# Weight mixing, the recurrent stage and the projections of a two-layer decoder as one program over shared buffers

## The chip, the cores and the metric

The kernel runs on one core of one Trainium2 chip. The metric is the device time of one execution in microseconds, lower is better. A core has five engines with an instruction stream each: PE (TensorE), DVE (VectorE), ACT (ScalarE), POOL (GpSimd) and SP (SyncE), which here does nothing but issue DMAs. The engines run side by side and wait for one another through semaphores.

## The reference

The reference is a decoder of two layers on `x` of 8 batches x 512 rows x 256 columns, all in float32. Each layer has three parts, and after each part comes `x = layernorm(x + part(x))`. Only the first layer's first two parts matter here:

```
# part 1: recurrence with weights mixed per batch
xn      = x * rsqrt(mean(x*x) + 1e-6) * norm_weight
probs   = softmax(mean(xn over rows) @ router_w.T + router_b)       # 8 experts, per batch
W_hg    = sum_e probs[e] * w_hg[e]    (512 x 256)                    # mixed weights, one set per batch
W_out   = sum_e probs[e] * w_out[e]   (256 x 256)
hidden, gate = split(xn @ W_hg.T)
h_t     = sigmoid(-gate_t) * h_(t-1) + sigmoid(gate_t) * g(hidden_t)  # scan over 512 rows
x1      = layernorm(x + (h @ W_out.T + x))
# part 2: cross attention, 16 heads of 16 columns; ctx is a second input
q, k, v = x1 @ Wq.T + bq, ctx @ Wk.T + bk, ctx @ Wv.T + bv
scores  = softmax(q k^T / 4); the 52 keys with the smallest column sums are dropped; out = scores v
```

Behind these come a routed feed-forward part and the whole second layer. They are not touched.

## The kernel before

The kernel is a row of stages. Each stage is a block with one instruction stream per engine. A stage allocates its buffers and semaphores through `Room` (line 25); when the stage ends, `Room.clear` frees the semaphores and puts a barrier over all engines, so nothing of the next stage starts before everything of this one, its last store included, is done.

**Mixing** (`stage_mix`, line 65). SP loads the eight batches of `x` into `x_all` and then twelve pieces of 512 KB of expert weights into `chunk` (L116). ACT forms the sums of squares, POOL the inverse roots `inv_all`, PE the means, and a small chain of tiny operations gives the router's shares. Then PE multiplies each weight piece with the shares (L213, 12 pieces of 8 matmuls), DVE (L182) and ACT (L129) copy the halves into `w_all`: the mixed weights of all batches, 128 partitions x 8 batches x 2 x 768.

**Recurrent stage** (`stage_rec`, line 217). It builds its own identity matrix, and copies the mixed weights of two batches at a time by DMA from `w_all` into `whg` and `wout` (L269, L272). ACT first issues eight stores of 1 MB of zeros into the scratch `buf` (L310) and then comes to its first work, `turned(0)` (L316). The engines then go through the batches in a written order, with a hardware loop for batches 2 to 5. For batch b, PE does: 8 matmuls for gate and hidden (L412, "gate(b)" in this text), 8 transposes of the next batch's normalized rows (L399, "turn(b+1)"), 8 matmuls for the output of the batch before (L423, "output(b-1)"). ACT does three sigmoids (L324 to L326) and copies the transposed rows out of PSUM (L316). DVE does: maximum (L347), the sum with `x` of batch b-1 (L352), product (L358), statistics (L362), scan (L370), variance (L376, L379), normalized rows of batch b+2 (L337), and the final layernorm of batch b-1 (L386). SP stores `x1` (L287).

**Projections** (`stage_proj`, line 444). SP loads the three weights and their biases and the first two batches of `x1` and of `ctx` (L469 to L477). For batch b, PE does: 8 transposes of the rows (L564), Q and K with 4 matmuls each (L571, "Q(b)", "K(b)"), V with 8 (L576, "V(b)"). ACT copies the transposed rows (L522), and writes Q and K in full and as a bf16 part (L529, L530) and later the middle bf16 part of the rest (L534). DVE subtracts: the rest (L544) and the low part (L547), and adds the bias to V (L550). SP, in a loop, waits until V(b) is done, loads the rows and the context of batch b+2, then waits for the low parts and stores Q and K (768 KB each, L482) and V (512 KB, L485). All of these go through SP's one DMA queue.

**Attention and routing** (`stage_attend_route`, line 659). Heads go by in chunks of four. `half_chunk` (line 760) loads a chunk's queries or keys with six DMAs of 64 KB (L765). SP issues the queries of chunk 0 and all of chunk 1, ACT the keys of chunk 0. PE waits for chunk 0 and for six constants of POOL, and then does the first scores (L1360). DVE waits for four fills of POOL first, and ACT's first `Exp` (L993) loads its table.

Of the kernel before, what the change touches and what calls it, by code (L numbers as in the profile page):

```python
# [14 lines left out]
P = 128  # L15
# [49 lines left out]
def stage_mix(nc, a, x_all, inv_all, w_all):  # L65

    KC = P // E
    C = 4  # L70
    G = 3 * D // (KC * C)
    with ExitStack() as ctx:
        r = Room(nc, ctx, "mix")
        junk = r.sb("junk", [P, B, T, D], BF16)
        ssq, msq = r.sb("ssq", [P, B, T]), r.sb("msq", [P, B, T])
        mhalf = r.sb("mhalf", [P, T])
        meanT = r.sb("meanT", [P, DH, B])
        nw = r.sb("nw", [P, DH])
        rwT = r.sb("rwT", [P, DH, E])
# [3 lines left out]
        prT = r.sb("prT", [E, B])  # L83
        prP = r.sb("prP", [P, B, 1])
        ident = r.sb("ident", [P, P])
        sel = r.sb("sel", [E, E, KC])
        mask = r.sb("mask", [P, KC])
        blocks = r.sb("blocks", [P, B, KC])
        chunk = [r.sb(f"chunk{g}", [P, C, D]) for g in range(G)]
        wide = r.sb("wide", [P, B, T, B])  # L90
        mean = r.sb("mean", [B, D])
        ps_sum = r.ps("ps_sum", [B, D])
        ps_mean = r.ps("ps_mean", [P, DH, B])
        ps_small = r.ps("ps_small", [P, 3, 8])
        ps_w = [[r.ps(f"ps_w{u}{h}", [P, C, B, KC]) for h in range(DH)] for u in range(2)]
        c_ld = r.sem("c_ld")
        x_ld, w_ld = [r.sem(f"x_ld{j}") for j in range(B // 2)], [r.sem(f"w_ld{g}") for g in range(G)]
        ssq_up, msq_up, inv_up, mean_up = (r.sem(n) for n in ("ssq_up", "msq_up", "inv_up", "mean_up"))
        const_up, soft_v, soft_s, soft_t = (r.sem(n) for n in ("const_up", "soft_v", "soft_s", "soft_t"))
        mixed, out_v, out_s = r.sem("mixed"), r.sem("out_v"), r.sem("out_s")  # L100
        wide_up = r.sem("wide_up")
# [3 lines left out]
        def _(sp):  # L105
# [9 lines left out]
            for g in range(G):  # L115
                sp.dma_start(chunk[g][:, :, :], a["L0_mix_w"][g].rearrange("p (c d) -> p c d", c=C)).then_inc(w_ld[g], 16)  # L116

        @block.scalar
        def _(act):
            for b in range(B):  # L120
# [5 lines left out]
            act.activation(ex[:, :], lg[:, :], ACT.Exp, bias=nmax[:, :], accum_out=esum[:, :]).then_inc(soft_s, 1)  # L126
            for g in range(G):
                act.wait_ge(mixed, g + 1)
                act.activation(w_all[:, :, 1, g * (C * KC):(g + 1) * (C * KC)].rearrange("p b (c k) -> p b c k", c=C),  # L129
                               ps_w[g % 2][1][:, :, :, :].rearrange("p c b k -> p b c k"), ACT.Copy).then_inc(out_s, 1)  # L130

        @block.gpsimd
        def _(pool):
            pool.memset(mhalf[:, :], -0.5).then_inc(const_up, 1)
            pool.memset(ident[:, :], 0.0).then_inc(const_up, 1)
            pool.memset(sel[:, :, :], 1.0).then_inc(const_up, 1)
            pool.wait_ge(const_up, 3)
            pool.affine_select(out=ident[:, :], in_=ident[:, :], compare_op=ALU.not_equal, fill=1.0, base=0,
                               pattern=[[-1, P]], channel_multiplier=1).then_inc(const_up, 1)

            pool.affine_select(out=sel[:, :, :], in_=sel[:, :, :], compare_op=ALU.is_equal, fill=0.0, base=0,
                               pattern=[[-1, E], [0, KC]], channel_multiplier=1).then_inc(const_up, 1)
            pool.memset(wide[:, :, :, :], 0.0).then_inc(const_up, 1)
            for b in range(B):
                pool.wait_ge(msq_up, b + 1)
                pool.tensor_tensor(inv_all[:, b, :], msq[:, b, :], mhalf[:, :], ALU.pow).then_inc(inv_up, 1)
# [2434 lines left out]
```

## Time and profile before

| | us |
|---|---|
| runs of the kernel before | 2081.13, 2084.89, 2091.33 (median 2084.89) |
| the profiled execution | 2084.87 |
| its span (first to last instruction in the trace) | 2083.1 |
| PE busy | 1843.2 (88%) |
| DVE busy | 1253.6 (60%) |
| ACT busy | 976.6 (47%) |
| POOL busy | 617.0 (30%) |
| moved by DMA | 189.5 MB |

The engines overlap, so the busy times don't add up to the span. The profiled execution's own time is 1.8 us above its span. The span begins with the mixing stage; the first scores of the attention stage are at 327.58 us, and everything behind them is some 1755 us of the span.

### The profile page before, as it was taken

What the parts mean: (1) busy time and instruction counts of PE and PEld (TensorE: products, weight loads), DVE (VectorE), ACT (ScalarE), POOL (GpSimd) and SP (SyncE); (2) the same over time, 40 slices, a digit from 0 to 9 for tenths busy, and PEclk for the clock granted to TensorE, in tenths of its full rate; (3) what the DMA queues carried; (4) which work ended last, traced back from release to release, by engine and by line L of the source; (5) the groups of instructions that cost most, each with busy time, mean ns of one, the idle gap of its engine ahead of it and who ended that gap; (6) DMA issues with size and microseconds to landing.
All of it is one profiled execution on the core that took longest, in us unless ns stands there. A gap on an engine that the chain in (4) does not pass through costs nothing. (4 is left out here: it accounts for less than half of the span.)

```text
span 2083.1 us, 26554 instructions
## 1 busy us (share of the span) xinstructions
PE 1843.2 (88%) x8441; PEld 1082.9 (52%) x8441; DVE 1253.6 (60%) x2929; ACT 976.6 (47%) x2530; POOL 617.0 (30%) x800
## 2 busy tenths in 40 slices
PE   7694885889988988889878999999689999999997
PEld 5352542445544545445445655656456565566553
DVE  2474444888899998999631121231566667675665
ACT  4230556998898989989322111111132223232210
POOL 2000004555576666766430001000433113211100
PEclk9897996999999999999999999999899999999999
DMA  5533554121222322221563344341421111100000
GB/s 202 218 110 94 206 206 99 53 62 51 67 77 65 88 62 82 75 76 59 185 211 111 101 133 139 112 142 51 142 62 50 48 39 46 46 5 21 11 11 21
DMA packets 168422, 189.50 MB, mean 91 GB/s; under 512 B 19908, under 2 KB 146107, under 8 KB 167264
## 3 DMA queue, kind: packets, MB, share of 16 engines
q1 hardware_dynamic: 160512, 162.90, 24.7%
q0 software_dynamic: 6144, 16.18, 2.5%
q10 hardware_dynamic: 1632, 8.78, 1.1%
q8 instruction: 66, 1.08, 0.2%
q14 instruction: 68, 0.56, 0.1%
HBM read 118.95 MB, written 63.18 MB: 87 GB/s over the span
## 5 line engine op out<-in xcount | busy, mean ns | idle before, releaser
L927 POOL TENSOR_SCALAR xa_probs<-xa_probs,xa_small 128x512 f32<-128x512 f32 x512 | 344.7, 689 | 253.0 <-DVE xa_small L1083 253.0
L993 ACT ACTIVATE xa_probs<-xa_ps_s,xa_small 128x512 f32<-128x512 f32 x512 | 360.8, 742 | 46.2 <-DVE xa_small L1089 41.3
L1089 DVE TENSOR_REDUCE xa_small<-xa_ps_s 128x2 f32<-128x1024 f32 x256 | 309.2, 1208 | 52.4 <-PE xa_ps_s L1360 52.3
L1371 PE MATMUL xa_ps_t<-xa_ident,xa_probs 128*128 128x128 f32 x2048 | 309.1, 284 | 17.2 <-DVE early L756 7.1
L1371 PEld LDWEIGHTS xa_ps_t<-xa_ident,xa_probs 128*128 128x128 f32 x2048 | 230.1, 143 | 153.1 <-ACT early L758 44.4
L2425 PE MATMUL ta_ps_e<-late,ta_x5T 128*128 128x512 f32 x512 | 243.9, 612 | 1.4 <-DVE ta_acc L2175 1.4
L1360 PE MATMUL xa_ps_s<-xa_k,xa_q 96*128 96x512 bf16 x512 | 159.8, 395 | 77.9 <-ACT xa_probs L993 56.2
L2175 DVE SCALAR_TENSOR_TENSOR ta_acc<-ta_ps_e,ta_gate,ta_acc 128x256 f32<-128x256 f32 x256 | 123.6, 483 | 101.4 <-PE ta_ps_e L2425 95.2
L1621 ACT ACTIVATE ex_hid<-ex_ps_g 128x512 f32<-128x512 f32 x64 | 38.2, 597 | 274.2 <-PE ex_ps_u L1718 271.3
L1672 DVE TENSOR_TENSOR ex_hid<-ex_hid,ex_ps_u 128x512 f32<-128x512 f32 x64 | 44.0, 688 | 182.6 <-ACT ex_hid L1621 177.1
L2425 PEld LDWEIGHTS ta_ps_e<-late,ta_x5T 128*128 128x128 f32 x512 | 98.5, 197 | 102.3 <-issue 87.4
L758 ACT ACTIVATE early<-xa_ps_t 128x512 f32<-128x512 f32 x216 | 135.4, 653 | 8.1 <-PE xa_ps_t L1371 7.8
L758 ACT ACTIVATE late<-xa_ps_t 128x512 f32<-128x512 f32 x216 | 133.9, 653 | 10.9 <-PE xa_ps_t L1371 10.8
L993 ACT ACTIVATION_READ_ACCUMULATOR xa_probs<-xa_ps_s,xa_small 128x1 f32 x512 | 133.7, 261 | 0.0
L1718 PE MATMUL ex_ps_g<-ex_xsT,early 128*128 128x512 f32 x256 | 120.4, 592 | 2.1 <-ACT ex_xsT L1603 2.1
L1718 PE MATMUL ex_ps_u<-ex_xsT,early 128*128 128x512 f32 x256 | 120.3, 592 | 0.0
L1360 PEld LDWEIGHTS xa_ps_s<-xa_k,xa_q 96*128 96x128 bf16 x512 | 35.6, 99 | 153.8 <-ACT xa_probs L993 92.3
L1728 PE MATMUL ex_ps_d<-early,ex_hid 128*128 128x256 f32 x512 | 113.4, 379 | 0.1
L1728 PEld LDWEIGHTS ex_ps_d<-early,ex_hid 128*128 128x128 f32 x512 | 96.0, 190 | 13.3 <-DVE ex_hid L1672 0.5
L1865 POOL DMA_INDIRECT ta_rows<-scratch_results,route_i x56 | 55.2, 985 | 90.7 <-POOLq L34 74.8
L1718 PEld LDWEIGHTS ex_ps_u<-ex_xsT,early 128*128 128x128 f32 x256 | 48.6, 190 | 61.2 <-issue 61.2
L1683 DVE COPY ex_out<-ex_ps_d 128x1024 f32<-128x1024 f32 x16 | 19.6, 1225 | 98.4 <-PE ex_ps_d L1728 98.4
(355 smaller groups left out, 3044.5 us busy)
## 6 DMA issues: line engine op xcount, KB each, us to landing
xa_q<-scratch_qk_parts SPq DMA_DIRECT2D x192, 64.0 KB
xa_k<-scratch_qk_parts SPq DMA_DIRECT2D x186, 64.0 KB
scratch_buf<-rec_zeros ACTq DMA_DIRECT2D x8, 1024.0 KB
early<-in_L_ffn_Wg SPq DMA_DIRECT2D x16, 512.0 KB
early<-in_L_ffn_Wu SPq DMA_DIRECT2D x16, 512.0 KB
early<-in_L_ffn_Wd SPq DMA_DIRECT2D x16, 512.0 KB
ex_xs<-scratch_buf SPq DMA_DIRECT2D x16, 512.0 KB, 5.2
scratch_results<-ex_out SPq DMA_DIRECT2D x16, 512.0 KB, 3.2
```

What stands on the lines that cost most here:

```text
L758: eng.activation(dst, src, ACT.Copy, accum_out=out).then_inc(copied[t], 1)
L927: ins = pool.tensor_scalar(probs[n % NP][:, t, :], probs[n % NP][:, t, :], rinv[n % 2][:, t:t + 1], 1.0, ALU.mult, ALU.mult)
L993: ins = act.activation(probs[n % NP][:, t, :], ps_s[j][:, t % 2, :], ACT.Exp, bias=nmax[n % 2][:, t:t + 1], accum_out=rsum[n % 2][:, t:t + 1])
L1089: dve.tensor_reduce(nmax[n % 2][:, 2 * j:2 * j + 2], ps_s[j][:, :, :], AX.X, ALU.max, negate=True).then_inc(max_up, 1)
L1360: ins = pe.matmul(ps_s[j][:, t % 2, :], q[c % 2][:, n % CH, t * P:(t + 1) * P], k_[c % 2][:, n % CH, :], start=True, stop=True)
L1371: ins = pe.transpose(ps_t[t % 2][:, i * P:(i + 1) * P], probs[m % NP][:, i, t * P:(t + 1) * P], ident[:, :])
L1672: dve.tensor_tensor(hid[m % 2][:, j, :], hid[m % 2][:, j, :], ps_u[j % 2][:, :], ALU.mult).then_inc(hid_up, 1)
L1718: ins = pe.matmul(ps[:, :], wt[:, h, j * P:(j + 1) * P], xsT[u][:, h, :], start=(h == 0), stop=(h == DH - 1))
L1728: ins = pe.matmul(ps_d[:, t, :], hid[u][:, j, t * P:(t + 1) * P], wd[u][:, j, :], start=(j == 0), stop=(j == FT - 1))
L1865: pool.indirect_dma_start(out=rows[b % 2][:, n, t, :], out_offset=None, in_=a["results"], in_offset=bass.IndirectOffsetOnAxis(ap=route_i[: ...
L2175: dve.scalar_tensor_tensor(acc[c % 2][:, t, :], ps_e[n % 2][:, i, :], gate[c % 2][:, t, e:e + 1], acc[c % 2][:, t, :], ALU.mult, ALU.add). ...
L2425: ins = pe.matmul(ps_e[n % 2][:, :, :].rearrange("p e d -> p (e d)"), x5T[c % 2][:, h, t * P:(t + 1) * P], ew[:, h, e:e + 2, :].rearrange( ...
```

## The change

`stage_mix`, `stage_rec` and `stage_proj` become one function, `stage_front`, with one block. The barriers and the clearing of semaphores between the three are gone, and the loops are written out batch by batch in Python, so every address is a constant. In detail:

- PE reads the mixed weights straight from `w_all`; the copies into `whg` and `wout` are gone. `late`, a buffer of 128 partitions x 64 KB that the later stages have anyway, holds the weight pieces first, and afterwards the projection's weights, rows, contexts and V. The bf16 parts and the full Q and K lie over `w_all`.
- `turn(0)`, its copy by ACT and a first `Sigmoid` for the table stand inside the mixing; rows 0 and 1 are normalized between the sums of squares.
- POOL fills the zeros after the mixing; SP, not ACT, stores them, 1 MB behind each store of `x1`.
- The projection's weights and the first two contexts are loaded after the mixing, the first two batches of rows behind the stores of `x1` of batches 2 and 3.
- PE's order at the seam is gate(7), output(6), turn_rows(0), K(0), output(7), Q(0), turn_rows(1), V(0); from then on K(b), Q(b), turn_rows(b+1), V(b). K goes before Q on ACT and DVE too.
- SP loads the context and the rows of batch b+1 (not b+2) just ahead of its stores of batch b, and so behind its stores of batch b-1. Behind the stores of batch 3 it loads the twelve pieces of the first query and key chunk of the attention stage (`ahead`).
- In the attention stage, chunk 0 is not loaded any more, ACT's table of `Exp` is loaded by a tiny activation, the wait of DVE for POOL's fills stands only before its first use, PE's wait for the constants before its first transpose, and POOL fills `vm` last.

The core of the diff (of `stage_front` only the parts that differ from the three stages; normalize to finish, rest, low and values do per batch what they did before):

```diff
+        chunk = [late[:, g * C * D:(g + 1) * C * D].rearrange("p (c d) -> p c d", c=C) for g in range(G)]
+        zeros = late[:, 12288:14336]
+        wq, wk, wv = (late[:, i * 512:(i + 1) * 512].rearrange("p (h n) -> p h n", n=D) for i in range(3))
+        ahead = first_chunk(late)
 @block.sync
+            def context(b):
+                wait(sp, pv_up, b - 1)
+                sp.dma_start(cT[b % 2], a["ctxT"][b].rearrange("(h p) s -> p h s", p=P)).then_inc(cT_ld[b % 2], 16)
+            def rows(b):
+                sp.wait_ge(x1_st[b % 2], 16 * (b // 2 + 1))
+                wait(sp, pt_up, b - 1)
+                sp.dma_start(x_in[b % 2], tok(a["x1"][b])).then_inc(x_in_ld[b % 2], 16)
+            def store(b):
+                sp.wait_ge(low_up, 2 * b + 2)
+                for n in range(2):
+                    sp.dma_start(a["qk_parts"][b, n]..., parts[n][b % 2]...).then_inc(qkv_st[b % 2], 16)
+                sp.wait_ge(v_up, b + 1)
+                sp.dma_start(tok(a["v"][b]), v[b % 2]).then_inc(qkv_st[b % 2], 16)
+            sp.wait_ge(mixed, G)
...
+            for b in range(2):
+                context(b)
+            sp.wait_ge(zero_up, 1)
+            for b in range(B):
+                sp.wait_ge(x1_up, b + 1)
+                sp.dma_start(tok(a["x1"][b]), x1[b % 2][:, :, :]).then_inc(x1_st[b % 2], 16)
+                sp.dma_start(buf[b], zeros).then_inc(zero_st, 16)
+                if b in (2, 3):
+                    rows(b - 2)
+            for b in range(B):
+                if b >= 1 and b + 1 < B:
+                    context(b + 1)
+                    rows(b + 1)
+                store(b)
+                if b == 3:
+                    sp.wait_ge(qkv_st[0], 48)
+                    for n in range(2):
+                        load_half(sp, a, ahead[n], 0, n, ahead_ld)
 @block.scalar
+            for b in range(B):
+                sigmoids(b)
+                if b + 1 < B:
+                    turned(b + 1)
...
+            rows_turned(0)
+            for b in range(B):
+                high(b, 1)
+                high(b, 0)
+                if b + 1 < B:
+                    rows_turned(b + 1)
+                middle(b, 1)
+                middle(b, 0)
 @block.tensor
+            for b in range(B):
+                gate(b)
+                if b + 1 < B:
+                    turn(b + 1)
+                if b >= 1:
+                    output(b - 1)
+            turn_rows(0)
+            project(0, 1)
+            output(B - 1)
+            for b in range(B):
+                if b >= 1:
+                    project(b, 1)
+                project(b, 0)
+                if b + 1 < B:
+                    turn_rows(b + 1)
+                project_v(b)
 stage_attend_route
-            half_chunk(sp, 0, 0)
             chunk(1)
-            pool.memset(vm[:, :, :, :, :], 0.0).then_inc(pad_up, 1)
-            half_chunk(act, 0, 1)
+            act.wait_ge(const_up, 1)
+            act.activation(warm[:, :], mhalf[:, 0:1], ACT.Exp)
-            dve.wait_ge(pad_up, 4)
-            pe.wait_ge(const_up, 6)
```

## Rows read from the trace of the kernel before

**Rows 1.** The page: busy time and instructions of each engine.
```profile
PE 1843.2 (88%) x8441; PEld 1082.9 (52%) x8441; DVE 1253.6 (60%) x2929; ACT 976.6 (47%) x2530; POOL 617.0 (30%) x800
```

**Rows 2.** Windows by stage: length, busy of each engine, PE clock, DMA share, GB/s.
```profile
29.00:53.80 24.80, 24.01 (x192) 23.82 (x192) 8.30 (x12) 7.16 (x12) 0.00 (x0) 0.90 0.12 47
53.80:67.66 13.86, 1.83 (x9) 1.49 (x9) 3.84 (x8) 1.39 (x3) 2.55 (x4) 0.64 0.84 330
67.66:185.10 117.44, 96.17 (x312) 56.54 (x312) 79.69 (x192) 32.05 (x39) 8.80 (x8) 0.94 0.31 118
185.10:202.75 17.65, 1.94 (x9) 1.57 (x9) 0.00 (x0) 1.23 (x2) 0.50 (x2) 0.50 0.68 201
202.75:311.30 108.55, 93.35 (x312) 55.47 (x312) 47.47 (x40) 61.12 (x87) 0.00 (x0) 0.97 0.56 194
311.30:327.58 16.28, 0.00 (x1) 0.04 (x2) 0.00 (x0) 1.28 (x1) 2.64 (x13) 0.50 0.89 191
```

**Rows 3.** Timeline, mixing's end to the second gate: start, duration, engine, line, operation.
```profile
53.06 0.69 DVE L182 COPY w_all<-mix_ps_w 128x512 f32<-128x512 f32 x1 [1.10 <-PE mix_ps_w L213]
57.43 8.77 ACTq L310 DMA_DIRECT2D scratch_buf<-rec_zeros  x8
67.66 2.90 PE L412 MATMUL rec_ps_h<-rec_xnT,rec_whg 128*128 128x512 f32 x3 [8.20 <-ACT rec_xnT L316]
76.67 1.03 ACT L324 ACTIVATE rec_val<-rec_ps_h 128x1024 f32<-128x1024 f32 x1 [7.85 <-PE rec_ps_g L412]
80.77 5.37 PE L412 MATMUL rec_ps_h<-rec_xnT,rec_whg 128*128 128x512 f32 x8 [3.27 <-ACT rec_xnT L316]
...
122.13 3.60 PE L412 MATMUL rec_ps_g<-rec_xnT,rec_whg 128*128 128x512 f32 x8
```

**Rows 4.** Timeline, the recurrent stage's end.
```profile
170.78 2.32 DVE L370 TENSOR_TENSOR_SCAN rec_h<-rec_keep,rec_val 128x512 f32<-128x512 f32 x2
173.20 5.68 PE L423 MATMUL rec_ps_o<-rec_wout,rec_h 128*128 128x256 f32 x16 [6.24 <-DVE rec_h L370]
183.64 1.38 DVE L386 TENSOR_SCALAR rec_x<-rec_z,rec_mv,rec_rstd 128x256 f32<-128x256 f32 x4 [1.12 <-POOL rec_rstd L302]
```

**Rows 5.** Timeline, the projections' last two batches and the first scores.
```profile
290.62 3.62 PE L576 MATMUL proj_ps_v<-proj_wv,proj_cT 128*128 128x256 f32 x16
293.25 1.07 ACT L534 ACTIVATE proj_partsq<-proj_restq 128x1024 bf16<-128x1024 f32 x1
294.07 1.04 PE L564 MATMUL proj_ps_t<-proj_ident,proj_x 128*128 128x128 f32 x8
295.63 1.00 ACT L522 ACTIVATE proj_xT<-proj_ps_t 128x1024 f32<-128x1024 f32 x1
300.30 3.60 PE L571 MATMUL proj_ps_k<-proj_cT,proj_wk 128*128 128x512 f32 x8
306.52 1.23 DVE L544 TENSOR_TENSOR proj_restk<-proj_fullk,proj_partsk 128x1024 f32<-128x1024 f32 x1 [2.21 <-ACT proj_partsk L530]
310.12 0.37 SPq L482 DMA_DIRECT2D scratch_qk_parts<-proj_partsq  x1
319.13 5.62 SPq L765 DMA_DIRECT2D xa_q<-scratch_qk_parts  x12
327.58 1.87 PE L1360 MATMUL xa_ps_s<-xa_k,xa_q 96*128 96x512 bf16 x4 [20.23 <-DMA xa_k<-scratch_qk_parts]
```

**Rows 6.** DMA issues of 188 to 330 us, with time to landing.
```profile
proj_x<-scratch_x SPq DMA_DIRECT2D x8, 512.0 KB, 4.0
```

**Rows 7.** One line (L116), the twelve weight pieces of 512 KB: time to landing.
```profile
DMA to landing us min/median/max: 11.9/13.0/14.5
```

**Rows 8.** Windows: one projection batch's transfers, the first chunks, low clock after idle PE.
```profile
170.80:177.00 6.20, 3.80 (x9) 3.11 (x10) 4.12 (x12) 0.00 (x0) 1.01 (x1) 0.50 0.00 0
217.50:226.10 8.60, 7.87 (x21) 3.95 (x22) 3.38 (x3) 3.80 (x7) 0.00 (x0) 1.00 1.01 360
321.00:327.60 6.60, 0.02 (x1) 0.06 (x2) 0.00 (x0) 1.28 (x1) 0.93 (x4) 0.50 1.18 139
```

More of the change, by code:

```diff
@@ L118, in _, with turned, sigmoids @@
         @block.scalar
         def _(act):
+            def turned(b):
+                act.wait_ge(t_up, b + 1)
+                wait(act, hg_up, b - 1)
+                for k in range(DH):
+                    ins = act.activation(xnT[b % 2][:, k, :], ps_t[:, k, :], ACT.Copy, scale=nw[:, k:k + 1])
+                ins.then_inc(xnT_up, 1)
+            def sigmoids(b):
+                act.wait_ge(hg_up, b + 1)
+                wait(act, h_up, b - 1)
+                act.activation(val[b % 2][:, :, :], ps_h[:, :, :], ACT.Sigmoid).then_inc(sig_up, 1)
+                act.activation(take[b % 2], ps_g[:, :, :], ACT.Sigmoid).then_inc(sig_up, 1)
+                act.activation(keep[b % 2], ps_g[:, :, :], ACT.Sigmoid, scale=-1.0).then_inc(sig_up, 1)
@@ L120, in _, with middle @@
+            def middle(b, n):
+                act.wait_ge(rest_up, 2 * b + 2 - n)
+                act.activation(parts[n][b % 2][:, 1, :, :], full[n][b % 2], ACT.Copy).then_inc(mid_up, 1)
             for b in range(B):
@@ L185, in _, with turn @@
+            dve.wait_ge(pc_ld, 96)
+            for b in range(B):
+                rest(b, 1)
+                rest(b, 0)
+                low(b, 1)
+                low(b, 0)
+                values(b)
         @block.tensor
         def _(pe):
+            def turn(b):
+                pe.wait_ge(xn_up, b + 1)
+                wait(pe, xnT_up, b)
+                for k in range(DH):
+                    for t in range(T):
+                        ins = pe.transpose(ps_t[:, k, t * P:(t + 1) * P], xn[b % 2][:, t, k * P:(k + 1) * P], ident[:, :])
+                ins.then_inc(t_up, 1)
@@ new lines, in gate @@
+            def gate(b):
+                pe.wait_ge(xnT_up, b + 1)
+                wait(pe, g_up, b)
+                wait(pe, sig_up, 3 * b)
+                if b == 0:
+                    pe.wait_ge(out_v, G)
+                    pe.wait_ge(out_s, G)
+                for out, first in ((ps_h, 0), (ps_g, DH)):
+                    for n in range(DH):
+                        for k in range(DH):
+                            ins = pe.matmul(out[:, n, :], w_all[:, b, k, (first + n) * P:(first + n + 1) * P], xnT[b % 2][:, k, :],
+                                            start=(k == 0), stop=(k == DH - 1))
+                ins.then_inc(hg_up, 1)
@@ new lines, in project @@
+            def project(b, n):
+                w, src, up = ((wq, xT[b % 2], q_up), (wk, cT[b % 2], k_up))[n]
+                if b == 0:
+                    pe.wait_ge(pc_ld, 96)
+                    pe.wait_ge(sig_up, 3 * B)
+                    pe.wait_ge(g_up, B)
+                if n == 0:
+                    pe.wait_ge(xT_up, b + 1)
+                else:
+                    pe.wait_ge(cT_ld[b % 2], 16 * (b // 2 + 1))
+                wait(pe, high_up, 2 * b - n)
+                for m in range(DH):
+                    for k in range(DH):
+                        ins = pe.matmul(ps_qk[n][:, m, :], w[:, k, m * P:(m + 1) * P], src[:, k, :], start=(k == 0), stop=(k == DH - 1))
+                ins.then_inc(up, 1)
@@ L187, in _, with project_v @@
+            def project_v(b):
+                if b == 0:
+                    pe.wait_ge(z_up, B)
+                wait(pe, v_up, b)
+                for t in range(T):
+                    for k in range(DH):
+                        ins = pe.matmul(ps_o[:, t, :], cT[b % 2][:, k, t * P:(t + 1) * P], wv[:, k, :], start=(k == 0), stop=(k == DH - 1))
+                ins.then_inc(pv_up, 1)
             pe.wait_ge(const_up, 6)
```

640 lines of the change are left out of this document (249 added, 391 removed).

## The prediction

> **What bounds the kernel now.** I read the page first, then windows by stage, then the timeline of the front, then the landings of its DMAs. On the page PE is busy 88% of the span [rows 1]; the attention and the later stages, some 1755 us, are not touched, so the question is how much of the front's 327.58 us is PE at work. The windows answer it [rows 2]. In the mixing PE is busy 24.0 of 24.8 us. From its end to the first gate matmul (13.86 us) it works 1.8 us; in the recurrent stage 96 of 117 us; from that stage's last layernorm to the first Q matmul (17.65 us) 1.9 us; in the projections 93 of 109 us; and from the last stores to the first scores (16.28 us) not at all. So three seams of 48 us together hold 3.8 us of PE's work. What ends each: at the first, ACT issues eight stores of zeros for 8.77 us before it copies the transposed rows [rows 3]; at the second, barrier, weight loads and row loads; at the third, the landing of the last stores, the barrier, and loads that end only at 327.58 [rows 5]. Inside the stages the loops run on PE and short waits.
>
> **The change part by part.** Times are in the trace's own span (2083.1 us; this execution took 2084.87, practically the median of 2084.89), and each step moves the chain.
>
> *First seam.* The last copy into `w_all` ends at 53.06 + 0.69 = 53.75. gate(0) then waits for nothing else: its rows are turned during the router chain, where PE and ACT idle. It starts at 53.8 and not 67.66: -13.9 us. It also starts right behind the mixing, at full clock. Before, gate(0) took from 67.66 to 76.6, its first matmuls 0.97 us each, against 2 x 3.6 = 7.2 us later, less 0.1 of overlap [rows 3]: -1.9 us. ACT's three sigmoids and the copy still stand between gate(0) and gate(1), so the dip of gate(1) (its first half 5.37 and not 3.60 us) may stay; I keep it, and count its 1.6 us as a bound. Sum -15.8 us.
>
> *The recurrent loop.* DVE's order per batch and PE's are the old ones, so the period stays. The 16 copies out of `w_all` fed nothing late; their removal is worth 0. The zero stores go to SP's queue: 1 MB at 360 GB/s [rows 8] is 2.9 us per batch of more than 12 us, hidden behind the loop; uncovered it would cost that much per batch, 23 us in all. The written-out code costs nothing: the mixing is written out already and PE is busy 24.0 of 24.8 us there [rows 2].
>
> *Second seam.* Scan(7) ended at 170.78 + 2.32 = 173.1 [rows 4], now 157.3. turn_rows(0) and K(0) fit in front of it. output(7) runs at full clock in 3.6 us, the duration of V, which has its shape [rows 5], and not in 5.7, which it took after 6.2 us of idle at half clock [rows 4, 8]: end 161.0. Then Q(0) to 164.6, turn_rows(1) to 165.6, V(0) 169.2, K(1) 172.8, Q(1) 176.4 (3.6, 1.04, 3.6 us [rows 5]). On DVE the last layernorm ended 6.1 us after output(7) (178.9 to 185.0 [rows 4]): 167.1. Two rests of 1.23 us: 169.6. From the end of the last rest to the store of Q and K it took 2.4 us (307.75 to 310.12 [rows 5]): store(0) is issued at 172.0.
>
> *A new loop.* Here the change adds a wait. SP issues in order, and rows(b+1) stands behind store(b-1). turn_rows(b+1) needs those rows; ACT's middle parts stand behind its copy of the turned rows; DVE's low parts need the middle parts; store(b) needs the low parts; rows(b+2) stands behind store(b). Waiting on PE behind turn_rows are V, the next K and Q. The old kernel loaded two batches ahead and before the stores. From turn_rows to its store: 1.04 + 1.00 + 1.07 [rows 5] + 2.4 + 0.3 for the hand-overs = 5.8 us. From the store's issue to the landing of the rows: the queue holds 768 + 768 + 512 KB of stores, then 512 KB of context, then the rows, 3.1 MB. The same 3.1 MB took 8.6 us before, with the DMAs fully busy (share 1.01) [rows 8]; what a load costs beside its bytes is 4.0 us, the landing of the rows on an empty queue [rows 6], less 1.4 us for 512 KB at 360 GB/s: 2.6. Sum 11.2, period 17.0 us, against 11.9 us of PE's work (3.6 + 3.6 + 1.04 + 3.62) and some 13 before (108.55 us for eight batches, the first partly at a low clock [rows 2]). In the gap of 5 us PE's clock may fall, as it did to 0.50 in the idle time before output(7) [rows 8]; turn_rows then takes about twice its 1.04 us, a period of 17.8 us. I take 17.2, a fall in one gap of four. Do the rows really wait for the bytes ahead of them? The twelve weight pieces of the mixing, as large as the rows and issued behind other loads, landed 11.9 to 14.5 us after their issue [rows 7], the rows on an empty queue after 4.0 [rows 6]. I take the queue as served in order. The bounds of the period are 11.9 (hidden) and 23.7 (PE at half clock throughout).
>
> The Trainium skill, "DMA: Bandwidth & Descriptors", section "Queues, rings and completion order", says that on each DMA engine the descriptors of one issuing engine's queue are consumed in ring order. It speaks against the change, and rows 7 agree; the sum by it is the one taken here, while 4.0 us as in rows 6 would give the first rival.
>
> So turn_rows(2) starts at 172.0 + 11.2 = 183.2, PE having stood since 176.4. Five more periods: 86.0. Ahead of context 5 and rows 5 the queue gets the first chunk, twelve DMAs in 5.62 us of issuing [rows 5], 786 KB at 139 GB/s [rows 8]: +5.7. turn_rows(7) is at 274.9. Behind it itself, V(6), K(7) and Q(7): 11.9 us, and 2.0 if 4 of them run at half clock: 288.8. The last matmul of Q or K ended at 303.90 and the store came at 310.12: 6.2, so 295.0. From there to the next stage 9.0 us as before (310.12 to 319.13 [rows 5]): 304.0.
>
> *Third seam.* The first scores find their chunk: 304.2, not 8.45 us after the stage's start. Of the 8.2 us saved the +5.7 above are given back. The table of `Exp` (ACT's 1.28 us in the last window [rows 2]) was covered by the load; its cover now is the first scores and DVE's maximum of them, so it costs 0, at most 1.28. PE's and DVE's waits for POOL's constants, which the load covered too, are moved behind the first scores: 0. Chunk 1 needs about the 8.45 us that chunk 0 needed; four heads, whose scores alone are 4 x 4 matmuls at 1.87 us per four, stand before its use: 0.
>
> Sum: 304.2 - 327.58 = -23.4 us; 2084.87 - 23.4 = **2061.5 us**. With full clock in the new loop (17.0 us, nothing at its end) the first scores are at 301.2, and with the dip of gate(1) gone at 299.6: 2056.9. With 17.8 us they are at 307.2: 2064.5. A start of the queue 0.5 us quicker or slower moves it by 3 us, a rate 10% lower by 5. The likeliest's own range is 2050 to 2072.
>
> **The rivals.**
> (a) *The row loads don't wait for the stores.* For it: the landing of 4.0 us [rows 6]; against: rows 7. The period is 5.8, then 2.3 until the rows are issued (four DMAs before them at 5.62/12 us each and a short wait for V's sum), then 4.0: 12.1; turn_rows(2) at 178.3, (7) at 178.3 + 60.5 + 5.7 = 244.5, the first scores at 244.5 + 11.9 + 6.2 + 9.2 = 271.8: 2029.1 us. Hidden entirely, at 11.9 us a period with turn_rows(2) at 176.4 and no charge for the chunk: 263.0, 2020.3 us.
> (b) *PE's clock.* The new gaps fall into every batch, and PE stays at half clock through Q, K, V and turn_rows: 23.7 us per batch, more than the DMA's chain. For it: after idle PE ran at 0.50 [rows 8], and gate(1) slowed too [rows 3]. Against: the window after the idle seam of 17.65 us averages 0.97 [rows 2], so full clock comes back under work. Then turn_rows(7) is at 183.2 + 118.5 = 301.7, the first scores at 301.7 + 23.7 + 6.2 + 9.2 = 340.8, +13.2: **2098.1 us, slower**. It decides from a period of about 21.5 us up.
> (c) *The change gives back what it takes.* The seams go, but the new loop costs 21 to 22 us a batch, because stores and loads that follow in one queue run below 360 GB/s (at 240 GB/s the 8.6 us are 13): 5 x 4.4 us more and 4.4 before the first, 2088 us, no change. Against: the same bytes ran at 360 before, mixed in the same way.
>
> **How the numbers follow.** Forecast 0.60, (a) 0.20, (c) 0.12, (b) 0.08. A measurement of this kernel tells a change from none at about 0.5%, 10.4 us, so faster means below 2074.5 and slower above 2095.3. The forecast's range and (a) lie below: faster 0.80, same 0.12, slower 0.08. The range runs from 2024 to 2078: it cuts off the hidden case, most of (c) and (b).
>
> **What would show it.** The first gate matmul near 54 us, at once at full clock; output(7) at 3.6 us. In the projections PE waits for a DMA of the rows before each turn_rows from batch 2 on, turn to turn 16 to 18 us, once about 23 (batch 5), and rows landing 7 to 9 us after their issue; with (a) they land after 4 and the period is near 12; with (b) the windows show a clock near 0.5 over the projections. First scores within 0.5 us of the stage's start, near 304 us. Everything behind it should keep its length (1755 us); if that grows, I am wrong about what the change touches.

## The result, and the profile after

The changed kernel takes 2057.26 us (median of four executions) against 2084.76 for the kernel before (2081.13 to 2091.33, four runs). Three of the four executions took 2056.47, 2057.01 and 2057.51 us; the fourth was disturbed and took 4657.62 us, and neither the ratio nor anything below rests on it. The ratio is 0.9875, with a 95% interval of 0.984 to 0.991. The whole interval lies below 1: the kernel is faster, by some 1.2%. The prediction was 2061.5 us, with 2024 to 2078 as its range.

The profiled execution of the changed kernel took 2057.51 us, its span 2055.5. The page's line of busy times answers to [rows 1].

```profile
PE 1844.1 (90%) x8441; PEld 1084.2 (53%) x8441; DVE 1249.7 (61%) x2929; ACT 976.9 (48%) x2532; POOL 615.1 (30%) x795
```

The same number of matmuls, the same busy time: the change computes nothing less, it moves work together. The windows of the front [rows 2], cut at the new seams (columns: window, length, busy time of PE, weight load, DVE, ACT and POOL with their instructions, PE clock, DMA share, GB/s):

```profile
29.00:51.76 22.76, 21.70 (x192) 21.54 (x193) 8.47 (x13) 8.60 (x14) 0.76 (x1) 1.00 0.06 22
51.76:148.81 97.05, 89.56 (x296) 52.05 (x297) 66.57 (x155) 30.98 (x39) 7.29 (x7) 0.96 0.33 113
148.81:173.40 24.59, 22.70 (x81) 13.59 (x79) 19.33 (x44) 11.31 (x16) 2.01 (x2) 1.00 0.61 230
173.40:275.54 102.14, 66.39 (x202) 41.58 (x201) 31.55 (x27) 41.19 (x59) 0.00 (x0) 0.85 0.60 184
275.54:294.73 19.19, 16.55 (x56) 11.04 (x56) 8.41 (x8) 9.75 (x13) 0.00 (x0) 0.91 0.33 110
294.73:303.66 8.93, 0.00 (x1) 0.03 (x2) 1.11 (x1) 0.04 (x1) 0.04 (x2) 0.65 0.71 235
```

Recurrent loop and seam are now one run of work right behind the mixing: from 51.76 to 173.40 PE idles some 9 us in 122. But in the fourth window, the new projection loop, PE works 66 of 102 us at a mean clock of 0.85. PE's own timeline says why (start, length, engine, line, operation, and in brackets the idle time before it and what ended it):

```profile
51.76 3.67 PE L467 MATMUL front_ps_h<-front_xnT,front_w_all 128*128 128x512 f32 x8 [0.83 <-DVE front_w_all L420]
62.96 6.55 PE L467 MATMUL front_ps_h<-front_xnT,front_w_all 128*128 128x512 f32 x8 [3.22 <-ACT front_xnT L260]
...
155.17 3.72 PE L476 MATMUL front_ps_o<-front_w_all,front_h 128*128 128x256 f32 x16 [1.89 <-DVE front_h L355]
...
169.92 3.60 PE L503 MATMUL front_ps_h<-late 128*128 128x512 f32 x8
181.34 1.97 PE L487 MATMUL front_ps_t<-front_ident,late 128*128 128x128 f32 x8 [7.82 <-DMA late<-scratch_x]
...
275.54 1.09 PE L487 MATMUL front_ps_t<-front_ident,late 128*128 128x128 f32 x8 [3.81 <-DMA late<-scratch_x]
276.47 5.30 PE L512 MATMUL front_ps_o<-late 128*128 128x256 f32 x16
...
303.66 1.87 PE L1337 MATMUL xa_ps_s<-late 96*128 96x512 bf16 x4 [11.56 <-PEq L34]
```

The first gate is at 51.76 instead of 67.66 [rows 3], output(7) at 155.17 instead of 173.20 [rows 4], the first scores at 303.66 instead of 327.58 [rows 5]. PE's waits between 150 and 303 us, by releaser (total, times, longest):

```profile
PE front_ps_t L487 <- DMA late<-scratch_x: 35.8, 6, 10.7
```

turn_rows(b) stands for the 8 transposes of the rows of batch b in the new projection loop. Every turn_rows from batch 2 on waits for its rows. turn_rows(2) to (7) start at 181.34, 199.23, 217.18, 239.29, 257.45 and 275.54: periods of 17.9, 17.95, 22.1, 18.2 and 18.1 us, where PE's work is 11.2 (measured in e5 below). The longest period is the one whose rows stand behind the first chunk. SP's queue in one period (L190 loads rows, L195 stores Q and K), and the chunk:

```profile
173.39 1.23 SPq L190 DMA_DIRECT2D late<-scratch_x  x1
187.73 0.95 SPq L195 DMA_DIRECT2D scratch_qk_parts<-front_w_all  x2
...
191.47 1.22 SPq L190 DMA_DIRECT2D late<-scratch_x  x1
...
224.99 8.64 SPq L88 DMA_DIRECT2D late<-scratch_qk_parts  x12
```

From turn_rows(2) to its store: 187.73 - 181.34 = 6.4 us. From there to turn_rows(3): 11.5 us. Of these 3.7 are issuing what stands ahead, and 7.8 are the landing of the rows, which was 4.0 us on an empty queue [rows 6].

### The profile page after: what moved, and what is told of

The parts are those of the page before. It is cut to its first block and busy times, and to the rows that moved or that the text cites. A ratio compares the mean times of both kernels' runs of the same rounds, so it can differ in the third digit from the quotient of the medians.

```text
span 2055.5 us, 26201 instructions
## 1 busy us (share of the span) xinstructions
PE 1844.1 (90%) x8441; PEld 1084.2 (53%) x8441; DVE 1249.7 (61%) x2929; ACT 976.9 (48%) x2532; POOL 615.1 (30%) x795
## 5 line engine op out<-in xcount | busy, mean ns | idle before, releaser
L1350 PE MATMUL xa_ps_t<-xa_ident,xa_probs 128*128 128x128 f32 x2048 | 309.9, 285 | 17.1 <-DVE early L736 7.1
L1337 PE MATMUL xa_ps_s<-xa_k,xa_q 96*128 96x512 bf16 x496 | 153.1, 391 | 53.2 <-ACT xa_probs L971 51.4
```

Of the source, the lines that this page charges most:

```text
L1337: ins = pe.matmul(ps_s[j][:, t % 2, :], q_[:, n % CH, t * P:(t + 1) * P], keys[:, n % CH, :], start=True, stop=True)
L1350: ins = pe.transpose(ps_t[t % 2][:, i * P:(i + 1) * P], probs[m % NP][:, i, t * P:(t + 1) * P], ident[:, :])
```

## The experiments

Nine kernels, e1 to e9, and the changed one once more (c_changed_again), in three groups: e1 to e4; the repeat and e5 to e7; e8 and e9. The kernel before was measured beside each group, with medians of 2079.71, 2080.43 and 2083.15 us, so a ratio compares better than two medians of different groups. No experiment puts one of the three seams back by itself: what each seam gave is read from the timelines, and the experiments are about the new loop, the clock and the written-out code. T2 and T7 stand for the starts of turn_rows(2) and (7); in the changed kernel T7 - T2 is 94.2 us, and in its second profile (c_changed_again) 94.7.

**e1: rows loaded two ahead.**
```diff
                 if b >= 1 and b + 1 < B:
                     context(b + 1)
-                    rows(b + 1)
+                if b + 2 < B:
+                    rows(b + 2)
                 store(b)
```


> The changed kernel, with SP issuing the load of rows(b+2) and not rows(b+1) ahead of the stores of batch b (the buffer is free by then). Theory (the new projection loop is bound by the row loads that stand in SP's queue behind the stores of the batch before): PE's waits for the row loads (35.8 us in six waits) go, turn_rows comes every 12 to 12.5 us instead of every 18.0; the context of batch 5 still stands behind the first chunk, so K(5) waits some 5 us. First scores at 268 to 272 us of the span instead of 303.7, the execution near 2022 to 2026 us. Rival 1 (the period is the sum of the DMA work and PE's clock, not the order): the period stays above 16 us, first scores above 290. Rival 2 (the context loads take the rows' place as the late ones): period 14 to 16, PE waits for the context before each K.

Measured: 2020.72 us, ratio 0.9716 (0.970 to 0.9733). No turn_rows waits any more; PE waits for the context instead (the wait between 155 and 241.3 us):
```profile
187.64 1.04 PE L488 MATMUL front_ps_t<-front_ident,late 128*128 128x128 f32 x8
PE front_ps_g L504 <- DMA late<-in_ctxT: 9.5, 3, 5.4
268.80 1.87 PE L1338 MATMUL xa_ps_s<-late 96*128 96x512 bf16 x4 [11.55 <-PEq L34]
```
T7 - T2 is 241.30 - 171.71 = 69.6 us against 94.2, and the first scores are 34.9 us earlier, 33.2 of it behind turn_rows(1). The period is 11.2 us only where no context is late, 13.9 on the mean, so the second rival holds in part: three contexts came late and not one. The forecast's mechanism is shown: the new loop's period is the wait of the rows behind the store. What is late next is the load that still stands behind it.

**e2: rows ahead of the context.**
```diff
-                    context(b + 1)
                     rows(b + 1)
+                    context(b + 1)
```


> The changed kernel, with the rows of batch b+1 issued ahead of its context (two lines of SP swapped). Theory (one queue, served in order): the rows lose one DMA of 512 KB in front of them, 1.4 us at 360 GB/s; the period falls from 18.0 to 16.6, first scores 6 x 1.4 = 8.4 us earlier, near 295.3, the execution near 2049. Rival (DMAs in flight share the bandwidth, the order doesn't matter): the rows land when all 3.1 MB have, period and first scores unchanged within 1 us.

Measured: 2039.8 us, ratio 0.9816 (0.980 to 0.9833); T7 - T2 is 85.8 us, 1.7 a batch less than 94.2. The first scores come at 290.35, 5 us earlier than expected, of which 3 lie ahead of turn_rows(0), where gate(1) has no slow half here. With 512 KB fewer ahead of them (1.4 us at the 360 GB/s of [rows 8]) the rows are that much earlier, as an order by bytes within one queue would have it. But this run does not show that order: SP also issues the rows 1.4 us sooner, because the issue of the context (1.36 us) no longer stands ahead, and from their issue they land after 7.0 to 8.2 us, outside the chunk's period, against 7.3 to 8.1 in the changed kernel. The shorter gap also lets the clock stay up in some gaps (turn_rows at 1.09 to 1.10 us in three of six):
```profile
185.24 1.31 SPq L190 DMA_DIRECT2D late<-scratch_x  x1
186.59 1.36 SPq L185 DMA_DIRECT2D late<-in_ctxT  x1
193.41 1.10 PE L487 MATMUL front_ps_t<-front_ident,late 128*128 128x128 f32 x8 [3.37 <-DMA late<-scratch_x]
230.50 1.97 PE L487 MATMUL front_ps_t<-front_ident,late 128*128 128x128 f32 x8 [9.63 <-DMA late<-scratch_x]
```

**e3: rows in POOL's queue.**
```diff
                     context(b + 1)
-                    rows(b + 1)
+            for b in range(2, B):                                    # on POOL
+                pool.wait_ge(v_up, b - 1)
+                pool.wait_ge(x1_st[b % 2], 16 * (b // 2 + 1))
+                wait(pool, pt_up, b - 1)
+                pool.dma_start(x_in[b % 2], tok(a["x1"][b])).then_inc(x_in_gp[b % 2], 16)
```


> The changed kernel, with the rows of batches 2 to 7 loaded by POOL's queue instead of SP's, released by the same events (V of the batch before the last summed, x1 stored, buffer read). Theory (the rows wait for what stands ahead of them in their own queue): in a queue of their own they land 4 to 6.5 us after issue although the same stores run, the period falls to 13 to 15.5 us, first scores at 282 to 290, the execution 2036 to 2044. Rival (it is the bytes of the DMA engines, whichever queue they come from): the rows land at about the same point, 16.5 to 18 us a period, first scores above 297.

Measured: 2031.01 us, ratio 0.9767 (0.9749 to 0.9785); first scores 280.71. PE then waits for the semaphore of that queue. Stores, context, rows and the turn they feed, in one period, and the row of the DMA issues of 172 to 253 us (count, KB, median to landing):
```profile
200.19 0.95 SPq L196 DMA_DIRECT2D scratch_qk_parts<-front_w_all  x2
201.68 1.24 SPq L199 DMA_DIRECT2D scratch_v<-late  x1
201.95 0.75 POOL L257 DMA_DIRECT2D late<-scratch_x  x1 [16.11 <-DVE late L390]
202.96 1.45 SPq L186 DMA_DIRECT2D late<-in_ctxT  x1
208.65 1.10 PE L495 MATMUL front_ps_t<-front_ident,late 128*128 128x128 f32 x8 [1.40 <-DMA late<-scratch_x]
```
```profile
late<-scratch_x POOLq DMA_DIRECT2D x5, 512.0 KB, 7.2
```
The first period is 17.1 us, the others 14.1 to 15.1: 15.1 on the mean, 2.9 less than in the changed kernel outside the chunk's period. But the rows land no faster for having a queue of their own: 7.2 us, where 4 to 6.5 were expected, against 7.8 behind the stores and 4.0 alone. The gain comes from the issue, 6.9 to 8.0 us after turn_rows and not 10.1 to 10.7: POOL waits for V of the batch behind whose stores the rows stood, and not for its low parts, nor for SP to issue four DMAs first. And a chunk of twelve DMAs in SP's queue no longer delays the rows: there is no period of 22 us. What shares the DMA engines with the rows pays for them: V's stores land after 8.4 us and the contexts after 8.6, 6.9 and 7.7 in the changed kernel. The reading that fits is that the landing is made by what the DMA engines move at the time, in whichever queue it stands, and that the queue's order decides when the rows get in line. It isn't shown to the end: no run has the load in POOL's queue with the DMA engines idle, so a part of the 7.2 us could be this queue's own.

**e4: no first chunk.** The wait for it goes with it, and the attention stage loads it itself, now with all twelve DMAs on SP's queue (in the kernel before ACT issued the six of the keys).
```diff
                 store(b)
-                if b == 3:
-                    sp.wait_ge(qkv_st[0], 48)
-                    for n in range(2):
-                        load_half(sp, a, ahead[n], 0, n, ahead_ld)
```


> The changed kernel without the early load of the first query and key chunk: the attention stage loads chunk 0 itself, on SP's queue, before chunk 1. Theory (a ledger of both sides): the long period of batch 5 falls from 22.1 to 18.0 us (-4.1), and the first scores wait again for their load, now twelve DMAs on one queue (+8.4 to +9.5 after the stage's start): net +4.3 to +5.4, first scores 308 to 309, the execution near 2062. Rival (the early load is free, the long period has another cause): +8.4 or more, first scores at 312 or later.

Measured: 2056.62 us, ratio 0.9893 (0.9876 to 0.9909). One of the six turns, the one behind which the long period was, and the first scores:
```profile
233.10 1.10 PE L482 MATMUL front_ps_t<-front_ident,late 128*128 128x128 f32 x8 [3.69 <-DMA late<-scratch_x]
...
303.61 1.89 PE L1333 MATMUL xa_ps_s<-xa_k,xa_q 96*128 96x512 bf16 x4 [18.91 <-DMA xa_k<-scratch_qk_parts]
```
The long period is gone (17.8 instead of 22.1), and from T7 to the first scores it takes 35.5 us instead of 28.1. The chunk's load ahead saves 7.3 us there and costs 5.5 of T7 - T2 (88.7 against 94.2); counted from turn_rows(1), the net is 1.9 us. The expectation, 4.3 to 5.4 us net and first scores at 308 to 309, missed: they came at 303.61, because turn_rows(1) started 1.9 us earlier here (160.25 against 162.16) and the net behind it is smaller. In the median the chunk's load is worth nothing that shows (ratio 0.9893 here, 0.9875 and 0.9886 for the changed kernel). It is worth that little because it is bought in the loop that is bound by DMA.

**c_changed_again: the changed kernel again**, beside the next three.

> The changed kernel unchanged, as the yardstick of this call. Both theories: first scores within 3 us of 303.7, turn_rows 18.0 us apart (22.1 once). The runs of the other experiments showed gate(1) without the half-clock stretch after the same 3.2 us gap of PE; if that stretch is chance, this run may lack it too and then everything behind is 2.9 us earlier.

Measured: 2056.6 us (2050.5 to 2060.7), ratio 0.9886 (0.9844 to 0.9928); first scores 304.60. Its first mixing pieces ran slow (3.28 and 2.40 us instead of 2.05 and 1.95), and gate(1) has the slow first half again:
```profile
27.84 3.28 PE L542 MATMUL front_ps_h<-late 128*128 128x128 f32 x16 [0.59 <-DVE late L416]
30.91 2.40 PE L542 MATMUL front_ps_g<-late 128*128 128x128 f32 x16
...
52.00 3.67 PE L467 MATMUL front_ps_h<-front_xnT,front_w_all 128*128 128x512 f32 x8 [0.83 <-DVE front_w_all L420]
63.20 6.75 PE L467 MATMUL front_ps_h<-front_xnT,front_w_all 128*128 128x512 f32 x8 [3.22 <-ACT front_xnT L260]
```

**e5: both loads ahead of the stores.** rows(2) before the loop, everything one batch earlier, the chunk behind the row loads.
```diff
+            rows(2)
             for b in range(B):
-                if b >= 1 and b + 1 < B:
-                    context(b + 1)
-                    rows(b + 1)
-                store(b)
-                if b == 3:
+                if b + 2 < B:
+                    context(b + 2)
+                if b + 3 < B:
+                    rows(b + 3)
+                if b == 6:
                     sp.wait_ge(qkv_st[0], 48)
                     ...
+                store(b)
```


> The changed kernel with SP's loop turned round: context and rows of the next batches go into the queue ahead of the stores (context b+2 and rows b+3 before the stores of b), and the first chunk behind the stores of batch 5, where no loads follow. Theory (all stalls of PE in the new loop come from loads behind stores or behind the chunk): no wait of PE for a DMA is left in the projections, turn_rows every 11.2 us from the second to the last (the two-ahead kernel had 11.19 wherever no context was late), first scores 67 + 27.5 us after turn_rows(1), at 253 to 256, the execution 2004 to 2010. Rival (the DMA engines are the next bound: 8.6 us of transfers per 11.2 us leave too little room, and the chunk delays the last stores): period 12 to 14, or the stage's end later than 20 us after turn_rows(7); first scores above 262.

Measured: 2004.99 us (2001.42 to 2008.56), ratio 0.9633 (0.9596 to 0.967). It beats both kernels, the changed one by some 52 us. A window of the loop, and the first scores:
```profile
172.00:227.67 55.67, 55.67 (x200) 34.23 (x198) 29.32 (x26) 37.90 (x55) 0.00 (x0) 1.00 0.90 307
254.05 1.86 PE L1339 MATMUL xa_ps_s<-late 96*128 96x512 bf16 x4 [11.57 <-PEq L34]
```
PE is busy 55.67 of 55.67 us at full clock, the period is 11.2 us. So the DMAs of one batch (now at 307 GB/s, share 0.90) do fit beside it; only their order had kept PE waiting.

**e6: turn(0) behind the mixing**, where PE meets it after the last piece; ACT's copy goes with it.
```diff
-            turn(0)        # in the router chain
             ...            # the twelve pieces
+            turn(0)
```


> The changed kernel with turn(0) on PE and the copy of its result on ACT moved back behind the mixing. The mixing of the changed kernel took 21.9 us from its first matmul to its last copy and not 24.7 as before, which I had not forecast. Theory (turn(0) keeps PE at work through the router chain, so the clock is full when the mixing starts): here the first two pieces run at half clock again (+2.0 us), and gate(0) starts 2.4 us later behind the last copy for turn(0) and its copy: gate(0) at 56 to 56.5 us instead of 51.8. Rival (the shorter mixing comes from other buffers and addresses): the pieces take 1.79 us each from the first on, gate(0) at 54 to 54.5.

Measured: 2058.33 us, ratio 0.9898 (0.9863 to 0.9934), not to be told from the changed kernel by its time.
```profile
29.10 3.78 PE L541 MATMUL front_ps_h<-late 128*128 128x128 f32 x16 [0.59 <-DVE late L416]
32.67 2.53 PE L541 MATMUL front_ps_g<-late 128*128 128x128 f32 x16
...
52.91 1.04 PE L454 MATMUL front_ps_t<-front_ident,front_xn 128*128 128x128 f32 x8
55.30 3.70 PE L467 MATMUL front_ps_h<-front_xnT,front_w_all 128*128 128x512 f32 x8 [1.36 <-ACT front_xnT L260]
```
The first gate comes 3.5 us later than in the first profile of the changed kernel: some 1.4 us for the turn and ACT's copy (2.4 were expected, and so 56 to 56.5), the rest the slow first pieces. Over all profiles, the first piece took 2.05 us in eight of the nine with turn(0) ahead (c_changed_again is the ninth), and the mixing began slowly in all three without it (this one, the kernel before, and e8, whose 192 matmuls took 23.34 us). The 0.9 us of work that fills an idle stretch of PE there mostly spares the low clock at the start of the mixing, though not always.

**e7: PE filled before gate(1).** Seven matmuls whose result is never read.
```diff
+                if b == 0:
+                    for i in range(7):
+                        pe.matmul(ps_o[:, i % 4, :], ident[:, :], x_all[:, 0, i % 4, :], start=True, stop=True)
```


> The changed kernel with seven extra matmuls (128 x 256, results never used) on PE in the gap between turn(1) and gate(1). Theory (a gap of PE of 3.2 us puts the clock at risk, and the stretch at half clock in gate(1) of the changed kernel's profile, 6.55 us for 3.6, came from it): gate(1)'s first half takes 3.6 to 3.7 us in every profile, worth 0 to 2.9 us against a profile with the dip. Rival (chance that has nothing to do with the gap): the dip can stand here too. The time differs from the changed kernel's by less than 3 us either way.

Measured: 2056.91 us, ratio 0.9891 (0.9851 to 0.9932).
```profile
59.26 3.19 PE L551 MATMUL front_ps_o<-front_x_all,front_ident 128*128 128x256 f32 x14
62.65 3.70 PE L467 MATMUL front_ps_h<-front_xnT,front_w_all 128*128 128x512 f32 x8 [0.20 <-ACT front_xnT L260]
...
152.01 5.41 PE L476 MATMUL front_ps_o<-front_w_all,front_h 128*128 128x256 f32 x16 [1.89 <-DVE front_h L355]
```
(The rows count each of these float32 matmuls twice, as they show the eight of output(7) as x16, so x14 are the seven.) No slow half, but the time is that of c_changed_again (2056.6). The slow half costs 3 us where it comes: turn_rows(0) starts at 148.81 and 149.25 in the two profiles with it, and at 145.2 to 145.8 in the profiles of e1 to e5 without it, after the same gap of 3.2 us. But here the first scores come at 303.19, only 0.5 us ahead of the changed kernel's. Of the 3.2 us at turn_rows(0) output(7) hands back 1.7: it ran at half clock, 5.41 us, where the changed kernel's took 3.72 behind the same gap of 1.89 us.

**e8: the kernel before, its loops written out**, nothing else (one of the four places):
```diff
-            with eng.Fori(1, B // 2 - 1) as i:
+            for i in range(1, B // 2 - 1):
```


> The kernel before with its four hardware loops (recurrent iterations on the engines, POOL's, SP's and the projections') written out, and nothing else: stages, barriers, copies of w_all and loads stay. Theory (the recurrent period fell from 12.56-12.68 to 12.27 us because the addresses became constants and the loop's own register work and branches went): period 12.2-12.4 us in the recurrent loop, first scores 2 to 3 us earlier, 2077-2079 us against 2080. Rival (the period fell because POOL and ScalarE have less to do in the changed kernel: no copies of the later w_all, no barrier reload): period stays at 12.5-12.7 us, time within 1 us of the kernel before. Second rival (more code to fetch): slower by a few us, visible as idle time of PE with PEq as its releaser. The 327.58 of the first scores then splits: what is left of -23.9 is the seams' alone.

Measured: 2082.99 us, ratio 0.9995 (0.9975 to 1.0014). Two turns of the recurrent loop of the kernel before, then gate(0) and two turns of this one and its first scores:
```profile
114.31 1.09 PE L399 MATMUL rec_ps_t<-rec_ident,rec_xn 128*128 128x128 f32 x8 [1.27 <-DVE rec_xn L337]
126.87 1.09 PE L399 MATMUL rec_ps_t<-rec_ident,rec_xn 128*128 128x128 f32 x8 [1.15 <-DVE rec_xn L337]
```
```profile
66.25 5.57 PE L412 MATMUL rec_ps_h<-rec_xnT,rec_whg 128*128 128x512 f32 x8 [8.42 <-ACT rec_xnT L316]
112.50 1.09 PE L399 MATMUL rec_ps_t<-rec_ident,rec_xn 128*128 128x128 f32 x8 [0.84 <-DVE rec_xn L337]
124.77 1.09 PE L399 MATMUL rec_ps_t<-rec_ident,rec_xn 128*128 128x128 f32 x8 [0.85 <-DVE rec_xn L337]
324.53 1.86 PE L1360 MATMUL xa_ps_s<-xa_k,xa_q 96*128 96x512 bf16 x4 [19.97 <-DMA xa_k<-scratch_qk_parts]
```
The period falls from 12.56 (up to 12.69 in other turns) to 12.27 us, exactly to that of the changed kernel (12.27): the theory on the period holds, the rival of fewer copies falls, since the copies are still there. The first scores are 3.05 us earlier, but not all of that is the loops': gate(0) starts at 66.25 and not 67.66, 1.4 us earlier, ahead of every loop that was changed. The recurrent loop gives 1.4 us and the projections 0.9; 0.7 is lost at the seam between them. The median does not show it, and the expected 2077 to 2079 us missed: the interval, 5.2 us down to 2.9 us up, holds both 3 us and nothing.

**e9: loads first and PE filled**, the ideas of e5 and e7 together.

> The kernel of e5_loads_before_stores with the seven extra matmuls of e7_pe_filled_before_gate1 (their result is never read). In e5 gate(1) ran its first half in 3.70 us without them, in the changed kernel in 6.55 and 6.75 us in two profiles. Theory (the half-clock stretch after the 3.2 us gap comes in some executions): with the gap filled it comes in none, first half 3.70 us, and the median is 0 to 3 us under e5's 2004.99, so 2002-2005 us, inside e5's interval. Rival (the extra matmuls delay gate(1)): 0.5-1 us slower than e5, gate(1) starting later than 11.2 us after gate(0). First scores at 253-255 us either way.

Measured: 2008.88 us (2006.33 to 2012.48, five runs), ratio 0.9659 (0.9633 to 0.9686), first scores 254.08. It is not faster than e5 alone; the expected 2002 to 2005 missed, and the filler is worth nothing measurable. Gate(1) started 11.2 us after gate(0), so the extra matmuls did not delay it; the kernel before was 2.7 us slower too in this group, and the intervals of the two ratios overlap.

## Why the prediction was right

The forecast was 23.4 us off the front, and the front lost 23.9. Step by step:

*First seam: right in kind, 2.0 us too small.* gate(0) followed the last copy at once, as said, but at 51.76 instead of 53.8: the mixing began at the same time and each piece took 1.79 us from the first on, where before the first two took 3.8 and 2.4 at low clock. e6 and the count of profiles beside it put that down to turn(0), which the forecast had moved there without asking what it does to PE's clock; it is 2 us in most executions, not in all. gate(0) ran at full clock, as forecast. The dip of gate(1) stayed and was larger: 6.55 us for its first half, 1.2 more than the 5.37 counted.

*The recurrent loop: the term of "nothing" was mis-sized.* The periods went from 12.56 to 12.69 us to 12.27, and from turn(2) to turn(7) it took 61.3 and not 62.7 us: 1.4 us in all. e8 gives the same 1.4 and puts it down to the written-out loop.

*Second seam: right here, in part by luck.* output(7) started at 155.17 (forecast 157.3), took 3.72 us (3.6), and store(0) was issued at 169.65 (172.0): the 2.3 us are those of the steps ahead. But full clock for output(7) holds in four of the ten profiles of the changed form (this one, the repeat, e2 and e3). In the other six it took 5.41 us after the same gap of 1.89 us, and turn_rows(1) came 15.0 us behind turn_rows(0) instead of 13.4.

*The new loop: the mechanism right, two sizes off.* From turn_rows to the store it took 5.5 us at full clock (5.8) and 6.4 at half; half clock came in four turns of six and not in one of four, together 1.1 us more than forecast in five periods. From the store's issue to the landing it took 11.5 to 11.8 (11.2), 2.1 us more in five. The period was 18.0 (17.2, and 17.8 with the slower turn). The chunk lengthened the landing of its period to 16.6 us, by 5.0 (5.7); by the periods alone it looks like 4.1, but the turn_rows ahead of it was one of the two at full clock. Together T7 came at 275.54 (274.9), and from there to the first scores it took 28.1 (29.3). The sum held also because errors cancelled: 2.3 us early at store(0), 0.5 late in the first landing, 1.1 and 2.1 late in the five periods, 0.7 back from the chunk and 1.2 behind T7.

The Trainium skill, "DMA: Bandwidth & Descriptors", section "Queues, rings and completion order", has the descriptors of one queue consumed in ring order on each DMA engine. e2 fits that, with 1.7 us for 512 KB fewer ahead, but 1.4 us of earlier issue would explain most of it as well, and the long landings of [rows 7] would come from engines shared by all that is under way, too. And e3 bounds what that order is worth: in another queue the same rows still took 7.2 us, not the 4.0 of the first rival. So the step "the queue is served in order" gave the right size, and whether for the right reason is not shown: the landing behind the stores is 7 to 8 us in either queue.

*Third seam: right.* Last store to next stage 303.62 - 294.73 = 8.9 us (9.0), first scores 0.04 us behind. The table of `Exp` and the constants cost nothing that shows.

*Behind the first scores: 1755.5 us before, 1751.8 after*, where the forecast had no change. These 3.7 us complete the 27.6 us of the two spans. They lie in a stretch where the same instructions ran more at half clock in the profile of the kernel before, for example at 3.41 and 1.84 us:
```profile
1512.54 3.41 PE L2340 MATMUL ta_ps_v<-late,ta_x4T 128*128 128x2 f32 x16
1427.58:1527.58 100.00, 78.74 (x275) 50.67 (x274) 41.42 (x93) 18.43 (x29) 27.05 (x23) 0.86 0.28 90
```
```profile
1487.05 1.84 PE L2319 MATMUL ta_ps_v<-late,ta_x4T 128*128 128x2 f32 x16
1403.66:1503.66 100.00, 79.97 (x290) 50.90 (x289) 43.32 (x96) 20.62 (x33) 30.34 (x26) 0.90 0.29 93
```
Whether this is the change's stays open. All ten profiles of the changed form have 1745.1 to 1752.5 us there, in no order by what was changed in the front; the two of the old form have 1755.5 and, in e8, 1760.9, and those two run alike in this stretch. Against a part of the change: both profiles are of executions above the median of their kernel (2087.15 us in e8, the longest of twelve with a median of 2082.99; 2084.87 for the kernel before, with 2079.71 to 2083.15 in the groups), and the medians fall by about what the first scores move, in e5 by 75.4 and 73.5 us, in e1 by 59.0 and 58.8.

*The rivals.* (a) fell: the rows do not land after 4 us while the stores run. What it priced can be had in another way: without the wait e5 ends at 2005, even under the 2020.3 given as the hidden case. Its first scores, 254.05, lie 9.0 us ahead of the 263.0 of that case: 3.5 because PE's floor is 11.2 us a batch and not 11.9 (the durations overlap by some 0.17 us each), 4.8 because turn_rows(2) can start at 171.6, 0.7 behind T7. The other 6 us are not the front's; the kernel before was 4.4 us lower beside e5 too. (b) fell: after a gap the clock came back within turn_rows and V (1.97 us, and 4.46 to 5.74 instead of 3.62), and K and Q ran at 3.60. (c) fell: the bytes went through at the forecast rate.

Where the rest went: with the loads ahead of the stores the change gives 23.9 + 49.6 = 73.5 us at the first scores (327.58 to 254.05). Two thirds were handed back, nearly all in the loop: from turn_rows(1) to (2) 19.2 us and T7 - T2 94.2, against 11.2 and 56.0 in e5. Not all of the 73.5 us are the seams': T7 - T2 was 65.4 us before. There PE waited in every batch for ACT's copy of the rows it had just turned (window 215 to 294), which the new order, turn_rows one batch ahead, spares it:
```profile
PE proj_ps_q L571 <- ACT proj_xT L522: 9.6, 6, 1.7
```

Open is why gate(1) has its slow half in both profiles of the changed kernel and in both of the old form, and in none of e1 to e6, with the same matmuls and the same 3.2 us gap before it; and why output(7) is slow in just six profiles.

## What to carry to other kernels

When stages are joined, read the issue order of each DMA queue as part of the dependence loop: a load that stands behind a store of results is as late as the results, and here a load one batch ahead, behind the stores, turned 11.2 us of work into a period of 18 us. Load as far ahead as the buffers allow, ahead of the stores in program order, and put a load for the next stage where the current one has no more loads to wait for. And read a gain in a profile against the scatter of the stretches behind it: 3 us gained in the front were invisible in 2083.

## What was unexpected of the hardware

- A queue of its own hardly shortened the landing: 512 KB took 4.0 us alone, 7.8 behind 2.5 MB in the same queue and 7.2 in POOL's queue beside SP's.
- The same gap of PE (3.2 us) was followed by matmuls at half clock in four profiles and at full clock in six others that lacked a filler (e1 to e6). A gap of 1.89 us before output(7) was followed by half clock in six profiles and by full clock in four. In e5 the granted clock was 1.00 in that gap (149.83 to 151.72) and 0.50 from 153.52 to 155.32, so it fell only when PE was at work again.
- The issue of a load of 512 KB on SP's queue took 0.39 to 0.46 us in the old loop, where the loads stood ahead of the stores, and 1.2 to 1.4 us behind stores in the new one; the twelve of the chunk took 8.64 us in the loop and 5.62 before [rows 5].
